# A four-stage transformer kernel on one core: Q's rows first in the opening, half of x normalised by ScalarE, work moved into the router's chain, and a bias added in sixteen pieces

## The reference

```python
x = x + cross_attention(layernorm(x), ctx)   # 16 heads of 16; q, k, v, softmax over 361 keys, Wo, bo
x = x + moe(layernorm(x))                    # router softmax, top 2 of 8 experts with a capacity, plus 0.1 * shared expert
x = x + bitnet_cross_attention(layernorm(x), ctx)   # ternary weights, 8-bit activations, two attention rounds, f1, relu, f2, b_f2
x = x + recurrent(layernorm(x))              # 16 steps of a gated cell, then tanh
```

## Time and profile before

| | us |
|---|---|
| median of three runs | 960.16 |
| the profiled execution | 962.21 |
| its span, first to last instruction | 960.4 |
| TensorE busy (8198 matmuls) | 794.5 (83%) |
| VectorE busy | 719.2 (75%) |
| ScalarE busy | 555.5 (58%) |
| GpSimd busy | 303.2 (32%) |
| mean granted clock of TensorE | 0.910 |

### The profile page before, as it was taken

How to read it: one execution, slowest core, us unless ns; L and a number is a source line. 1 busy time by engine, 2 the same in 40 slices (tenths; PEclk the granted TensorE clock), 3 DMA queues, 4 the chain that set the end, 5 groups by cost and what they waited for, 6 DMA issues and landing times.

```text
span 960.4 us, 22060 instructions
## 1 busy us (share of the span) xinstructions
PE 794.5 (83%) x8198; PEld 583.8 (61%) x8198; DVE 719.2 (75%) x1456; ACT 555.5 (58%) x1150; POOL 303.2 (32%) x246
## 2 busy tenths in 40 slices
PE   3678888898898768879889999996555999869995
PEld 1355666666665545667657777783213777449994
DVE  7788777878887998767586666655696998767865
ACT  6356766666665436634366555636797776672532
POOL 6156453444551506031232220003641111243400
PEclk9799999999999776989999999997555999889998
DMA  6423443334443246404176654454210000200002
GB/s 169 102 66 82 107 101 98 104 93 114 119 114 85 80 143 224 160 25 133 37 208 185 179 168 146 123 135 140 65 47 10 1 2 1 89 1 2 3 2 69
DMA packets 76898, 89.53 MB, mean 93 GB/s; under 512 B 22150, under 2 KB 64929, under 8 KB 76826
## 3 DMA queue, kind: packets, MB, share of 16 engines
q1 hardware_dynamic: 69994, 80.50, 30.4%
q0 software_dynamic: 6144, 7.42, 3.0%
q10 hardware_dynamic: 688, 0.66, 0.3%
HBM read 72.87 MB, written 15.43 MB: 92 GB/s over the span
## 4 chain that ended last, share of the span: by engine, by line
PE 49%; DVE 27%; ACT 9%; issue 7%; DMA 4%; SPq 1%; POOL 1%; ACTq 0%; another core or an unknown queue 0%; DVEq 0%
PE ps L1183 11%; PE ps L1170 9%; PE ps L557 3%; PE ps L357 3%; PE ps L455 3%; PE ps L529 3%; DVE p L545 2%; PE ps L599 2%; DVE m L515 2%; PE ps L2195 2%; PE ps L510 2%; DMA k_parts<-kp 2%; DVE pmax L1652 2%; PE ps L2206 2%; DVE area L1778 1%
## 5 line engine op out<-in xcount | busy, mean ns | idle before, releaser
L515 DVE TENSOR_REDUCE m<-ps 100x2 f32<-100x722 f32 x128 | 115.6, 904 | 48.4 <-PE ps L510 46.5
L536 ACT ACTIVATE p<-ps 128x800 f32<-128x800 f32 x128 | 106.8, 834 | 42.6 <-PE ps L529 39.8
L1232 ACT ACTIVATE hT<-ps,cols 128x500 f32<-128x500 f32 (+1 forms) x96 | 62.5, 651 | 107.8 <-PE ps L1170 94.4
L1183 PE MATMUL ps<-w_h,hT_h 128*125 128x256 f16 (+1 forms) x384 | 105.5, 275 | 7.4 <-DVE x L1279 6.8
L1239 DVE TENSOR_TENSOR hT_l<-hT,hT_h 128x500 f16<-128x500 f32 (+1 forms) x96 | 62.3, 652 | 60.9 <-ACT hT_h L1233 59.2
L545 DVE SCALAR_TENSOR_TENSOR p<-p 128x600 f32<-128x600 f32 x128 | 107.2, 839 | 0.0
L1183 PE MATMUL ps<-w_h,hT_l 128*125 128x256 f16 (+1 forms) x384 | 105.4, 274 | 0.0
L1183 PE MATMUL ps<-w_l,hT_h 128*125 128x256 f16 (+1 forms) x384 | 105.4, 274 | 0.0
L1075 POOL DMA_INDIRECT xe<-tokens,slot_of x32 | 44.5, 1391 | 154.4 <-PE ps L1193 100.7
L1170 PE MATMUL ps<-xe_h,w_h 128*128 128x500 f16 (+1 forms) x192 | 72.5, 378 | 13.8 <-ACT hT_h L1233 5.6
L529 PE MATMUL ps<-qs,ks 128*128 128x100 f16 x768 | 63.0, 211 | 15.9 <-ACT p L536 15.1
(11 more groups left out here) (344 smaller groups left out, 2128.0 us busy)
## 6 DMA issues: line engine op xcount, KB each, us to landing
sw<-in_L_ffn_w_dram SPq DMA_DIRECT2D x16, 512.0 KB
sw<-in_L_ffn_w_dram SPq DMA_DIRECT2D x8, 1024.0 KB, 5.8
k_parts<-kp SPq DMA_DIRECT2D x32, 192.0 KB, 2.7
ks<-k_parts SPq DMA_DIRECT2D x32, 192.0 KB
stage<-in_L_xattn_W_f_dram SPq DMA_DIRECT2D x6, 1024.0 KB
ctx_f<-in_ctxT_dram SPq DMA_DIRECT2D x16, 270.8 KB, 3.2
stage<-in_ctxT_dram SPq DMA_DIRECT2D x8, 541.5 KB
area<-in_ctxT_dram SPq DMA_DIRECT2D x16, 270.8 KB, 6.2
```

Of the source, the lines that this page charges most:

```text
L515: v.tensor_reduce(m32[p][:, 2 * i:2 * i + 2], ps[0:T, at:at + 2, 0:KV], AX.X, ALU.max).then_inc(m_max, 1)
L536: s.activation(p32[:, i % HALF, :, :, :].rearrange("p j n t -> p n j t"), ps[:, t_bank(i):t_bank(i) + 2, 0:(KJ + 1) * T].rearrange("p n (j ...
L1183: i = pe.matmul(bank[4 + j % 3][0:m, 0:C], hTp[p][hh][:, f, j * m:(j + 1) * m], w2p[of][ww][:, f, :], start=(f == 0 and hh == ww), stop=(f ...
L1232: s.activation(hT[:, f % 3, 0:m], bank[2 + f % 2][:, 0:m], ACT.Silu, bias=bias, scale=1.0 / WS)
```

## The change

1. SyncE's order in the opening: all of x is loaded early; K's first half, then Q's store, then their loads; Wo is loaded after Wv has landed, which lets the split of Wv wait for Wv alone; K's second batch, the contexts and the rest follow.
2. Groups 2 and 3 of x are normalised by ScalarE as x * rstd + (-mean * rstd). VectorE makes the shift (`open_shift`). A dummy exp stands before them.
3. `open_turn` of group 1 is before the scores, those of 2 and 3 behind pairs 1 and 4. `m_tensor` is behind pair 4. The bias row is made in bank 6 (OB_) in two parts behind the sixth and seventh pair and is spread behind the eighth.
4. The copy of the upper rows of ks on ScalarE stands directly behind Q of batch 0.
5. `fill` gets the low parts 4 to 7 of block 1, the four outputs of block 0, the sum of the weights' totals and the turn of block 2; VectorE's step of block 0 is empty.
6. b_f2 is added in 16 parts of 100 x 256, one behind each unit's normalisations; f12 of the unit after next stands before it.

```diff
+        def bias_row_tensor(pe, part):
+            pe.wait_ge(wvo_in, 32)
+            for k in range(2 * part, 2 * part + 2):
+                pe.matmul(OB_[0:1, 0:C], bv_col[:, k:k + 1], w_in_["Wo_heads"][0][:, k, :], start=(k == 0), stop=False)
+            if part == 1:
+                pe.matmul(OB_[0:1, 0:C], ones_row[:, 0:1], bo_row[:, :], start=False, stop=True).then_inc(yb_mm, 1)
+        def open_shift(v, g):
+            of = slice(LB * g, LB * (g + 1))
+            v.wait_ge(ln_std, g + 1)
+            vs.inc(v.reciprocal(rstd[:, of], stddev[:, of]))
+            vs.sync(v)
+            v.scalar_tensor_tensor(vareps[:, of], meanvar[:, of, 0], -1.0, rstd[:, of], ALU.mult, ALU.mult
+                                   ).then_inc(ln_rec, 1)
+        def open_norm_scalar(s, g):
+            s.wait_ge(ln_rec, g - 1)
+            for b in range(LB * g, LB * (g + 1)):
+                s.activation(xn[:, b, :], x[:, b, :], ACT.Identity, scale=rstd[:, b:b + 1], bias=vareps[:, b:b + 1]
+                             ).then_inc(ln_xn, 1)
...
-                v.wait_ge(w_in[name], 32 if name == "Wv" else 16)
+                v.wait_ge(w_in[name], 16)
...
+            if is_shared(n) and n == 0:
+                return
...
-                if at >= 17 and (at - 17) % 4 == 0 and (at - 17) // 4 < HF:
+                if at >= 17 and (at - 17) % 4 == 0 and (at - 17) // 4 < FC:
                     low_vector(v, 1, 1, (at - 17) // 4)
+                if at in (35, 39, 43, 47):
+                    out_vector(v, 0, 0, 0, (at - 35) // 4)
+                if at == 41:
+                    total_vector(v)
+                if at == 48:
+                    turn_vector(v, 2, 0)
...
-            for pair in range(B // 2):
...
+            def half_sum(u):
+                pair, r = unit_of(u)
+                if r == 0 and u < UNITS:
+                    tok = pair_tokens(pair)
+                    wait(g, n_s, 2 * (u - 1))
+                    g.tensor_tensor(f12[u % 2], fused[:, 0, tok], fused[:, 1, tok], ALU.add).then_inc(n_f, 1)
+            half_sum(0)
+            half_sum(1)
+            for u in range(UNITS):
+                half_sum(u + 2)
+                g.wait_ge(n_p, 2 * u + 2)
+                x_b2_gpsimd(g, u)
...
+            g.tensor_tensor(x[:, n, :], x[:, n, :], f2_b[:, :], ALU.add).then_inc(x_bias, 1)
...
-            open_norm(v, 2)
+            open_shift(v, 2)
+            open_shift(v, 3)
+            open_low(v, 1)
             for i in range(NP):
                 s_vector(v, 0, 0, i, 2 * (i % 2))
-                if i == 1:
-                    open_norm(v, 3)
-                if i == 2:
-                    open_low(v, 1)
+                if i in (2, HALF + 1):
+                    open_low(v, 2 + i // HALF)
...
             q_scalar(s, 0, 0)
+            s.wait_ge(k_pad, 2)
+            s.copy(ks_flat[1][64:128, :].bitcast(F32), ks_flat[0][64:128, :].bitcast(F32)).then_inc(set_s, 1)
             s.wait_ge(a_pad, 2)
             q_scalar(s, 1, 1)
+            open_std(s, 1)
             v_scalar(s, 0, 0, 0, bank[4])
             v_scalar(s, 0, 0, 1, bank[5])
...
             open_std(s, 3)
+            s.activation(avg_q[0:T, 1, 0:1], eps_col[:, :], ACT.Exp)
             open_high(s, 1)
+            for g in range(2, LG):
+                open_norm_scalar(s, g)
+            open_high(s, 2)
             for c in range(2):
                 c_scalar(s, 2, 0, 1, c)
+            s.wait_ge(s_pad, 1)
             m_scalar(s, 0, 0)
+            open_high(s, 3)
+            s.wait_ge(yb_mm, 1)
+            s.copy(ybias[:, :], OB_[0:1, 0:C]).then_inc(yb_ev, 1)
             q_scalar(s, 2, 0)
+            s.wait_ge(yb_mm, 2)
+            s.copy(ybias_b[:, :], OB_[0:T, 0:C]).then_inc(yb_ev, 1)
...
-            k_store(sp, 0, 0, 0, 0)
-            x_load(2)
-            k_store(sp, 0, 0, 0, 1)
+            for c in range(CC):
+                k_store(sp, 0, 0, 0, c)
+            k_load(sp, 0, 0, 0)
+            q_store(sp, 0, 0, 0)
+            sp.wait_ge(sel_in, 64)
+            q_load(sp, 0, 0, 0)
+            k_load(sp, 0, 0, 1)
+            q_load(sp, 0, 0, 1)
+            k_store(sp, 1, 0, 1, 0)
+            sp.wait_ge(wvo_in, 16)
             raw = w_in_["Wo_heads"][0]
             sp.dma_start(raw[:, :, :], a["L0_xattn_Wo_heads"].rearrange("(k p) n -> p k n", k=raw.shape[1])
                          ).then_inc(wvo_in, 16)
-            k_load(sp, 0, 0, 0)
-            k_load(sp, 0, 0, 1)
-            x_load(3)
-            k_store(sp, 1, 0, 1, 0)
+            k_store(sp, 1, 0, 1, 1)
             context_load(sp, 2, 0)
-            k_store(sp, 1, 0, 1, 1)
-            q_store(sp, 0, 0, 0)
```

More of the change, by code:

```diff
@@ L551, in pv_tensor @@
                 wait(pe, o_32, b)
+            if g == 0 and is_first(b):
+                pe.wait_ge(yb_ev, 2)
             pe.wait_ge(a_cv, NP * b + 2 * (g + 1))
@@ L1341, in step_vector @@
             q = 1 - p
-            before = HF if is_shared(n) and n == 0 else 0
+            if is_shared(n) and n == 0:
+                return
             if is_shared(n) and n == 1:
@@ L1353, in step_vector @@
             for f in range(FC):
-                if has_block(n, 1) and f >= before:
+                if has_block(n, 1):
                     low_vector(v, n + 1, q, f)
@@ L1918, in last_norm @@
         def last_norm(e, g):
-            e.wait_ge(ln_rec, g + 1)
+            e.wait_ge(ln_rec, 2 + g + 1)
             for b in range(LB * g, LB * (g + 1)):
@@ L2475, in _ @@
             s.wait_ge(const_in, 112)
+            open_std(s, 0)
             k_scalar(s, 0, 0, 0)
             k_high(s, 0, 0)
-            open_std(s, 0)
             k_scalar(s, 0, 0, 1, OB_)
@@ L2547, in _ @@
             v_tensor(pe, 0, 0, 1, None, bank[5])
+            open_turn(pe, 1)
             pe.wait_ge(q_32, 2)
-            pe.wait_ge(wvo_in, 32)
-            for k in range(HG):
-                pe.matmul(UB_[0:1, 0:C], bv_col[:, k:k + 1], w_in_["Wo_heads"][0][:, k, :], start=(k == 0), stop=False)
-            pe.matmul(UB_[0:1, 0:C], ones_row[:, 0:1], bo_row[:, :], start=False, stop=True).then_inc(yb_mm, 1)
             pe.wait_ge(s_pad, 1)
@@ L2556, in _ @@
                 s_tensor(pe, 0, 0, 0, i, 2 * (i % 2), i - 1)
-                if i == 0:
-                    pe.wait_ge(yb_ev, 1)
-                    pe.matmul(UB_[0:T, 0:C], ones_row[:, 0:T], ybias[:, :], start=True, stop=True).then_inc(yb_mm, 1)
-                if i in (1, HALF, NP - 1):
-                    open_turn(pe, (1, HALF, NP - 1).index(i) + 1)
-                if i == HALF + 1:
-                    m_tensor(pe, 0, 0, (yb_ev, 2))
+                if i == HALF:
+                    m_tensor(pe, 0, 0, None)
+                if i in (HALF + 1, HALF + 2):
+                    bias_row_tensor(pe, i - HALF - 1)
+                if i == NP - 1:
+                    pe.wait_ge(yb_ev, 1)
+                    pe.matmul(OB_[0:T, 0:C], ones_row[:, 0:T], ybias[:, :], start=True, stop=True).then_inc(yb_mm, 1)
+                if i in (1, HALF):
+                    open_turn(pe, (1, HALF).index(i) + 2)
             q_tensor(pe, 2, 0, (m_l, 1))
@@ L2597, in _ @@
             sp.dma_start(ctx_f32[1][:, :, :], ctx_d[1]).then_inc(ctx_in[1], 16)
-            x_load(1)
+            for g in range(1, LG):
+                x_load(g)
             sp.wait_ge(a_pad, 2)
@@ L2610, in _ @@
                          ).then_inc(wvo_in, 16)
-            k_load(sp, 0, 0, 0)
-            k_load(sp, 0, 0, 1)
-            x_load(3)
-            k_store(sp, 1, 0, 1, 0)
+            k_store(sp, 1, 0, 1, 1)
             context_load(sp, 2, 0)
-            k_store(sp, 1, 0, 1, 1)
-            q_store(sp, 0, 0, 0)
-            sp.wait_ge(sel_in, 64)
-            for c in range(CC):
-                q_load(sp, 0, 0, c)
             context_load(sp, 3, 1)
```

27 lines of the change are left out of this document (2 added, 25 removed).

## The result

| | before | after |
|---|---|---|
| median, us | 960.23 (958.5 to 963.38, 4 runs) | 947.39 (945.61 to 947.93, 4 runs) |
| the profiled execution, us | 962.21 | 947.37 |
| its span, us | 960.4 | 945.5 |
| VectorE busy, us | 719.2 | 708.9 |

The ratio is 0.9869, 95% interval 0.9844 to 0.9894: 12.8 us faster, with 13.4 forecast. When the changed kernel was timed again (label after_again, the last experiment), the ratio was 0.9879, interval 0.9847 to 0.9911.

A forecast was written before the change was run, and what follows sets the result against it. No engine is full over the whole span; each stage has its own limiting chain. Opening 6.0, router 3.2 and layer 2's bias 4.2 sum to 13.4 us: profiled 962.21 to 948.8, timed forecast 946.8 us, range 942.0 to 953.5.

The forecast's parts named there:

- Opening, 6.0 forecast: Opening: batch 0's first exp starts at 48.8 instead of 54.95 us, 6.0 us gained; bounds 7.5 and 2.
- The steps down to the first maximum: Opening: Q's store at 24.9 us, eight ScalarE normalisations of 0.51, group 1's low part to 34.15, then the maxima.
- The bias matmuls lie in TensorE's waits for VectorE: Opening's score loop: the bias row's matmuls fit into TensorE's waits; maximum 7 ends at 46.0 us.
- nearly idle before 17 us: Opening: DMA is nearly idle before 17 us and takes the early loads of x there.
- Q's store and ScalarE's normalisations as carriers: Opening: Q's earlier store readies the scores' operands seven us earlier; ScalarE's chain, with 4.1 us of normalisations, is then followed.
- Rival 1: Opening: SyncE's queue delays the row of maxima to about 52 us; opening gives 2, 950.8 us; chance 14%.
- Router, 3.2 forecast: Router: TensorE gets 5.1 us ahead, less 1.9 for a clock drop: 3.2 us gained; bounds 5.1 and 0.5.
- The step behind it: Router: block 2's turn, at step 48 of VectorE's chain, ends at 412.7 us; TensorE idles from 409.4 until then.
- The half clock: Router: TensorE's drop, as long as the old 6.8 us at the lower clock, costs 1.9 us.
- Rival 2: Router: half clock through two windows takes the gain; router gives 0 to 0.5, 949.7 us; chance 12%.
- Layer 2's bias, 4.2 forecast: Layer 2's attention: sixteen additions of 0.59 us remove three stretched normalisations, 4.2 us gained; bounds 5.2 and 2.7.
- The SBUF rule: Layer 2's bias: first issuer holds the shared pair for its whole instruction; sixteen pieces of 0.59 could exceed what is removed.

The follow-up runs named there:

- experiment 3: Changed kernel with the bias row moved out of the score loop, behind batch 0's first steps: 957.78 us, ratio 0.9938 to the kernel before.
- experiment 8: Changed kernel with last two bias pieces earlier, bias row in batch 0, and GpSimd's three high parts behind the second all-reduce: 956.55 us, ratio 0.9938 to before.
- experiment 5: Changed kernel with Q's store and loads back at the end of SyncE's list: 947.08 us, ratio 0.9877 to the kernel before.
- experiment 4: Changed kernel with groups 2 and 3 of x normalised by VectorE again instead of ScalarE: 951.47 us, ratio 0.9899 to the kernel before.
- experiment 7: Changed kernel with GpSimd's three high parts of the cell's weights moved behind the second all-reduce: 952.37 us, ratio 0.9900 to before; its second kernel is one_each.
- one_each: Changed kernel with the last two bias pieces earlier and one of GpSimd's three high parts behind the second all-reduce: 943.92 us, ratio 0.9835 to before.

## Why the prediction was right

**The sum.** 13.4 us were forecast and 12.8 measured, but not by the forecast's steps alone. From the means of the stages: opening 5.3, router 4.3, attention 4.4, less 3.0 at the first all-reduce, and 1.0 back before the second: 12.0.

**Opening, 6.0 forecast.** The first exp comes at 50.8 us on the mean of seven kernels with the new opening and at 54.4 on three with the old: 3.6. Another 1.7 lies in the batch loop (282.4 on the mean against 284.1), for which no step of the forecast stands and no experiment was made. The two groups overlap (281.7 to 284.3 and 283.1 to 285.1), so it may be scatter; the sum of 5.3 reached its size partly by that, which is luck. The steps down to the first maximum were right: Q's store at 24.75 (24.9 forecast), the maximum at 34.33 (34.15), eight normalisations of 0.505 (0.51). The step that failed is "The bias matmuls lie in TensorE's waits for VectorE": they take 1.87 us (at half clock), 1.19 and 0.59, and VectorE waits behind them. From maximum 5 to maximum 7 the changed kernel needs 4.64 us, and 2.77 where the row is elsewhere (experiments 3 and 8): 1.9 us. The place is still the cheaper of the two tried.

Three reasons were wrong too, without changing the number. DMA is not nearly idle before 17 us: its engines are 69% busy or more in every 2 us from 2 to 12 us and idle only from 12 to 18. The early loads of x were issued by 8.9 us, in the busy part. The forecast also followed Q's store and ScalarE's normalisations as carriers; experiments 5 and 4 take each away, and nothing is lost that the first exp shows. Probably one engine's slack covers the other's each time; both together were not taken away. What the runs leave as the carrier is the early load of x, which halves K's store, together with TensorE's turn of group 1 ahead of the scores and the table load ahead of the loop; these were not taken apart. Rival 1 (SyncE's queue) did not come: the row of maxima was issued at 44.04 (46 forecast).

**Router, 3.2 forecast, 4.3 measured.** The mechanism holds; the term, 5.1 less 1.9, was sized too low. The step behind it is the turn of block 2: it was to end at 412.7, which is 407.6 with the 5.1 us of lead that the router starts with, and it ends at 405.65 + 0.98 = 406.63 (L1237). That 1.0 us is the difference, and it shortens TensorE's new idle stretch too, from the 3.3 us computed to 2.21. The half clock came back as foreseen, 3.4 us of it, just behind that stretch. Rival 2 (the clock takes it) predicted 0 to 0.5.

**Layer 2's bias, 4.2 forecast, 4.4 in its stage.** Sixteen pieces of 0.73 (0.59 forecast), no normalisation above 0.413. The SBUF rule that the prediction weighed is met by its other side in experiment 7: the additions that lie beside normalisations stretch four of them from 1.38 to 4.07 us. By the Trainium skill, "SBUF — State Buffer", section "Who interferes with whom", the one that comes second waits for the whole instruction of the first. The trace agrees: in one_each the one stretched normalisation starts at 849.94, 0.15 us after an addition, and takes 1.15 us, until just behind the addition's end, where the other three take 0.40.

What the forecast did not see is the price behind the stage: it asked what each piece lies beside, and not what GpSimd does next. That was the all-reduce, and 3.0 us went there. The trace of the kernel before could have told: the same gap of 5.86 us stands before its second all-reduce. 1.0 us came back before the last norm. 0.6 of it stands in front of the second all-reduce, where GpSimd's work starts 7.4 us into the stage instead of 7.8, no longer behind the weights' transfer; for the rest the rows give no cause. The term was worth about 2.4 and not 4.2; the router's 1.1 above its forecast made up for most of it, and the batches' 1.7 for what the first exp lacked. So the nearness of 13.4 to 12.8 is luck in part: the first exp gave 2.4 us too little and layer 2's bias 1.8, the router gave 1.1 too much and the batches 1.7.

## What to carry to other kernels

When work is moved to the end of an engine's list, look at the next instruction of that engine too, above all where it is of another kind. Experiment 3 shows it a second time: a bias row made later held up a context's low parts on GpSimd, and those held up K. When an edit has several parts, take away one at a time: here the queue order and the second engine's share were each worth nothing beside the others. A bank that is freed earlier can be worth more than the operation that frees it, as the router shows.

## What the runs showed of the hardware

GpSimd's all-reduce starts 5.7 to 6.3 us after the end of an ordinary operation where its operand is ready by then (5.92, 5.71, 5.86, 5.75, 6.27 in the rows above). The next ordinary operation starts 6.7 to 7.4 us behind the second all-reduce (6.76, 7.08, 7.38), and 7.9 to 9.0 us behind the first, where its other waits may count too. In the kernel before, 23 us of idleness covered the gap at the first all-reduce. Not every change of operation has it: in the changed kernel the all-reduce at 671.95 starts 0.04 us behind an indirect DMA of GpSimd, and the next indirect DMA starts 0.17 us behind that all-reduce. By the Trainium skill, "GPSIMD Engine Reference", section "2.1 Instruction dispatch", the first call of a freshly loaded kernel pays about 6 us for loading code. The trace agrees with the size, and shows such a gap at both all-reduces and on the way back, not only once; that it is a load of code no row shows.

ScalarE's table load at 31.45 us takes 1.28, and its next operation starts at 32.74, 1.29 us after the load began. By the Trainium skill, "ScalarE: Activation LUTs", section "What ACT_TABLE_LOAD costs", a drain of about 1.38 us follows the load; here too the measurement differs, and there is none.
